# Re-dealing the lead-in of a transformer block: norm tiles, gates, gathers and an on-chip placement of the last tile

## What is computed

```python
x = x + L0_conv(ln_c(x))     # deformable attention with depthwise 3x3 convolutions
t = to_tokens(x); t = t + L0_ffn(ln_t(t)); x = from_tokens(t)
x = x + L1_conv(ln_c(x))     # large depthwise kernels, folded into one 7x7
t = to_tokens(x); t = t + L1_ffn(ln_t(t)); x = from_tokens(t)
```

## Time and profile before

| | us |
|---|---|
| median of 3 runs (least, most) | 1711.93 (1710.65, 1713.68) |
| the profiled execution | 1717.21 |
| its span, first to last instruction | 1715.4 |
| TensorE busy in it | 1422.9 (83%) |
| VectorE busy | 979.1 (57%) |
| ScalarE busy | 701.8 (41%) |
| GpSimd busy | 275.8 (16%) |

### The profile page before, as it was taken

The page is one execution under the profiler, slowest core; times in us unless marked ns, Lnnn a source line. Parts: engine busy times, 40 slices in busy tenths (PEclk is TensorE's granted clock), DMA queues, the critical chain, the costliest instruction groups (busy, mean ns, idle before and its releaser), DMA issues.

```text
span 1715.4 us, 19469 instructions
## 1 busy us (share of the span) xinstructions
PE 1422.9 (83%) x6076; PEld 958.6 (56%) x6076; DVE 979.1 (57%) x2678; ACT 701.8 (41%) x1433; POOL 275.8 (16%) x190
## 2 busy tenths in 40 slices
PE   4302528798777999998887999999999999999998
PEld 2201326555454577665555577666766676665565
DVE  4988777649896534448896544443434352244323
ACT  3210224335543234454543344454445443355443
POOL 2342115311162000001154000000000000000000
PEclk9999658898888999999888999999999999999999
DMA  3531304131342421331342422342224321221211
GB/s 100 129 95 46 105 20 116 53 111 57 90 120 52 122 67 51 95 112 61 106 103 59 129 67 52 93 120 70 71 64 114 98 66 48 71 69 42 69 61 45
DMA packets 169448, 137.96 MB, mean 80 GB/s; under 512 B 114688, under 2 KB 163074, under 8 KB 168962
## 3 DMA queue, kind: packets, MB, share of 16 engines
q1 hardware_dynamic: 162802, 131.26, 28.1%
q0 software_dynamic: 3072, 4.82, 1.2%
q10 hardware_dynamic: 3472, 0.63, 0.2%
HBM read 97.02 MB, written 39.65 MB: 80 GB/s over the span
## 4 chain that ended last, share of the span: by engine, by line
PE 50%; issue 19%; DVE 12%; POOL 8%; ACT 5%; DMA 3%; SPq 2%; ACTq 1%; POOLq 0%; DVEq 0%
PE y_ps L917 19%; PE at_ps L1020 8%; POOL pix_mem L837 6%; PE h_ps L926 5%; PE h_ps L925 5%; PE h_ps L924 5%; DVE vq_mem L1195 4%; PE at_ps L973 3%; POOL ln_rstd L824 3%; ACT ln_cen L689 2%; PE lb_ps L894 2%; PE lg_ps L907 1%; DVE part L1151 1%; DVE kon_mem L1195 1%; ACT hidden L784 1%
## 5 line engine op out<-in xcount | busy, mean ns | idle before, releaser
L784 ACT ACTIVATE hidden<-h_ps,b 128x448 f32<-128x448 f32 x672 | 424.6, 634 | 716.9 <-PE h_ps L926 714.0
L917 PE MATMUL y_ps<-hidden,w 128*96 128x448 f32 x1344 | 638.0, 559 | 29.6 <-ACT hidden L784 21.3
L924 PE MATMUL h_ps<-xh,w1h 96*128 96x448 f32 x672 | 474.4, 706 | 0.0
L1151 DVE SCALAR_TENSOR_TENSOR part<-y_ps,b,gate_t 96x448 f32<-96x448 f32 x224 | 151.8, 678 | 512.4 <-PE y_ps L917 472.4
L824 POOL TENSOR_TENSOR ln_rstd<-ln_ve,minus_half 112x4 f32<-112x4 f32 x112 | 156.0, 1393 | 1208.9 <-DVE ln_ve L1134 1208.7
L917 PEld LDWEIGHTS y_ps<-hidden,w 128*96 128x96 f32 x1344 | 207.4, 167 | 105.0 <-ACT hidden L784 59.5
L925 PE MATMUL h_ps<-xl,w1h 96*128 96x448 f32 x672 | 250.7, 373 | 0.0
L926 PE MATMUL h_ps<-xh,w1l 96*128 96x448 f32 x672 | 249.2, 371 | 0.0
L924 PEld LDWEIGHTS h_ps<-xh,w1h 96*128 96x128 f32 x672 | 130.5, 194 | 139.2 <-issue 122.9
L925 PEld LDWEIGHTS h_ps<-xl,w1h 96*128 96x128 f32 x672 | 131.8, 196 | 120.5 <-issue 119.7
L689 ACT ACTIVATE ln_cen<-ln_cen,ln_rstd 112x96 f32<-112x96 f32 x448 | 130.2, 363 | 160.7 <-POOL ln_rstd L824 160.5
(11 more groups left out here) (133 smaller groups left out, 1248.9 us busy)
## 6 DMA issues: line engine op xcount, KB each, us to landing
gate_t<-gates_dram SPq DMA_DIRECT2D x112, 336.0 KB, 3.1
value_pairs<-pix_mem SPq DMA_DIRECT2D x56, 168.0 KB, 3.1
x_mem<-norm_c SPq DMA_DIRECT2D x16, 420.0 KB, 4.2
x_mem<-norm_a SPq DMA_DIRECT2D x16, 336.0 KB, 3.8
ln_x<-in_x SPq DMA_DIRECT2D x28, 168.0 KB, 2.5
norm_a<-ln_cm SPq DMA_DIRECT2D x28, 168.0 KB, 2.3
res_mem<-in_x SPq DMA_DIRECT2D x4, 1176.0 KB, 9.8
x_attn<-res_mem SPq DMA_DIRECT2D x16, 294.0 KB, 2.9
```

The costliest lines, as they stand in the source:

```text
L784: act.activation(hidden[c % HID_RING][:, :], h_ps[c % H_BANKS][:, 0:TILE], ACT.Gelu, bias=b1[l][:, c:c + 1]).then_inc(gelu_done, 1)
L917: pe.matmul(y_ps[e % Y_BANKS][0:C, 0:TILE], w2[l][:, c, :], hidden[c % HID_RING][:, :], start=(j == 0), stop=(j == CPE - 1)).then_inc(hid_ ...
L924: pe.matmul(ps, hi, xh[:, ring(k)], start=True, stop=False)
L1151: dve.scalar_tensor_tensor(part[:, e, :], y_ps[e % Y_BANKS][0:C, 0:TILE], b2[l][:, e:e + 1], gate_t[e // 2][:, e % 2, :], ALU.add, ALU.mul ...
```

## The change

1. Lead-in: 13 steps in place of 15. Tiles 0 to 4 of a2 are normalised in steps 7 to 10, f0's tiles 0 to 3 in steps 10 to 12, f0's tiles 4 to 6 in (0, 0) and (0, 1), a2's tiles 5 and 6 in (0, 1) and (0, 2). Stage 3 of image 1 moves from step 13 to step 12. The first gate half is read in the last lead step, the second in (0, 1).
2. f0's tiles are turned in from `x_res` on the chip, once the strips they cover are added; they are no longer loaded. `x_res` of image 1 is loaded at stage 5 in place of 4, once all of them are turned.
3. The last tile of images 0, 2 and 3 goes from `ln_cm` straight into `xq` in three DMAs (`direct`); the fourth quarter's load leaves its rows out and is two DMAs.
4. In lead steps the second job's turn-in stands at chunk 8 (was 6), behind the first one's turn-back, and its apply at 9 (was 8).
5. Gathers: 4 in stage 3, 4 and 5 in stage 4, 3 in stage 5.
6. Ten of ScalarE's first loads go to SyncE's queue (4 ahead of the pads, 6 after step 0), four more to SyncE after step 1. `expand_w_out`, `spread_w_out` and `fold_taps` stand at the end of lead step 8.

```diff
-NORM_SLOT = {0: ("a", 2), 1: ("c", 0), ...
+NORM_SLOT = {1: ("c", 0), ...
-LEAD = 15
-START_JOBS = {... 6: [("a1", 5), ("a1", 6)], 11: [("f0", 0), ("f0", 1)], 12: [("f0", 2), ("f0", 3)],
-              13: [("f0", 4), ("f0", 5)], 14: [("f0", 6), ("a2", 0)]}
+LEAD = 13
+START_JOBS = {...
+              (-1, 6): [("a1", 5), ("a1", 6)], (-1, 7): [("a2", 0)], (-1, 8): [("a2", 1), ("a2", 2)],
+              (-1, 9): [("a2", 3)], (-1, 10): [("a2", 4), ("f0", 0)], (-1, 11): [("f0", 1), ("f0", 2)],
+              (-1, 12): [("f0", 3)], (0, 0): [("f0", 4), ("f0", 5)], (0, 1): [("f0", 6), ("a2", 5)],
+              (0, 2): [None, ("a2", 6)]}
-              11: [(1, 2)], 13: [(1, 3)]}
+              11: [(1, 2)], 12: [(1, 3)]}
...
-GATE_STEP = {(-1, LEAD - 2): (0, 0), (-1, LEAD - 1): (0, 1),
+GATE_STEP = {(-1, LEAD - 1): (0, 0), (0, 1): (0, 1),
...
-        TURN_IN = 1, 6
+        TURN_IN, LEAD_TURN_IN = (1, 6), (1, 8)
-        LEAD_APPLY, LEAD_BACK, LEAD_MOVE, LEAD_SCORES, LEAD_LATE_MOVE = (3, 8), 8, 9, 10, 4
+        LEAD_APPLY, LEAD_BACK, LEAD_MOVE, LEAD_SCORES, LEAD_LATE_MOVE = (3, 9), 8, 9, 10, 4
...
+                    if direct(job):
+                        for g in range(G):
+                            sp.dma_start(xq[Q - 1::Q, g, LAST_ROW * SIDE:LAST_ROW * SIDE + TILE],
+                                         ln_cm[job.n % 2][32 * g:32 * g + 32, :]).then_inc(xq_direct, 16)
+                        return
...
+                for r0, r1 in ((0, LAST_ROW), (ROWS_A - PAD_A, ROWS_A)) if split else ((0, ROWS_A),):
...
                 if 0 in stages and slot >= 0:
+                    load_quarter(stages[0], 2)
                     load_quarter(stages[0], 3)
...
-                if 4 in stages:
-                    b = stages[4]
+                if any(stage == (5 if b == 1 else 4) for stage, b in stages.items()):
+                    b = stages[5 if 5 in stages and stages[5] == 1 else 4]
...
+                    if b == 1:
+                        for job in PLACED:
+                            if from_attn(job):
+                                sp.wait_ge(ln_turned, job.n + 1)
...
                 if 4 in stages:
-                    gather(stages[4], 2, 6)
+                    gather(stages[4], 4, 8)
                 if 5 in stages:
-                    gather(stages[5], 10, 2 * GQ)
+                    gather(stages[5], 13, 2 * GQ)
                 if 1 in jobs:
                     scale_rows(jobs[1])
                 if 3 in stages:
-                    gather(stages[3], 0, 2)
+                    gather(stages[3], 0, 4)
                 if 4 in stages:
-                    gather(stages[4], 6, 10)
+                    gather(stages[4], 8, 13)
...
+                src = ln_x[n % 2]
+                if from_attn(job):
+                    src = x_res[:, tile_cols(job.tile)]
+                    pe.wait_ge(at_free, AT["attn", 0] + AT_Y + -(-(job.tile + 1) * TILE // YCOL))
+                else:
+                    pe.wait_ge(ln_loaded[n % 2], loads(n))
...
-                if (slot, p) == (1, 0):
+                if (slot, p) == (-1, 8):
+                    expand_w_out()
                     fold_taps()
```

More of the change, by code:

```diff
@@ L78 @@
 for _slot, _p in STEPS:
-    if _slot < 0:
-        _todo = [(what[0], int(what[1]), tile) for what, tile in START_JOBS.get(_p, [])]
+    if _slot < 0 or (_slot, _p) in START_JOBS:
+        _todo = [what and (what[0][0], int(what[0][1]), what[1]) for what in START_JOBS.get((_slot, _p), [])]
     elif _p <= 2:
@@ L88 @@
     JOBS[_slot, _p] = []
-    for _place, (_kind, _image, _tile) in enumerate(_todo):
+    for _place, (_kind, _image, _tile) in [(i, what) for i, what in enumerate(_todo) if what]:
         _job = Job(len(PLACED), _place, "f" if _kind == "f" else "c", _image, _tile,
@@ L376, in metaformer_kernel @@
         Q_ROUNDS = {4: (0, 9)}, {4: (0, 5), 5: (5, 8), 6: (8, 9)}
-        TURN_IN = 1, 6
+        TURN_IN, LEAD_TURN_IN = (1, 6), (1, 8)
         APPLY, BACK, MOVE, SCORES = 6, 7, 8, 9
         LATE_APPLY, LATE_BACK, LATE_MOVE, LATE_SCORES = 1, 2, 3, 5
-        LEAD_APPLY, LEAD_BACK, LEAD_MOVE, LEAD_SCORES, LEAD_LATE_MOVE = (3, 8), 8, 9, 10, 4
-        const_count, taps_count = [0], [0]
+        LEAD_APPLY, LEAD_BACK, LEAD_MOVE, LEAD_SCORES, LEAD_LATE_MOVE = (3, 9), 8, 9, 10, 4
+        const_count = [0]
         BAND_TILES = [3, 4, 6, 7]
         QUARTER_TILES = [2, 4, 6, 7]
+        XQ_LOADS = [sum(Q + (image in DIRECT) for image in range(b + 1)) for b in range(NB)]
+        LAST_ROW = PIX // TILE * TILE // SIDE - (Q - 1) * QROWS - TILE // SIDE + PAD_A
         CONV_STORE, ACC_LOAD = {}, {}
@@ L393, in norm_stores, with direct, from_attn, loads @@
         def norm_stores(norm, parity, tiles=TILES):
-            return 16 * sum(job.norm == norm and job.n % 2 == parity and job.tile < tiles for job in PLACED)
+            return 16 * sum(job.norm == norm and not direct(job) and job.n % 2 == parity and job.tile < tiles for job in PLACED)
+        def direct(job):
+            return job.norm is not None and job.norm[0] == "a" and job.norm[1] in DIRECT and job.tile == TILES - 1
+        def from_attn(job):
+            return job.kind == "f" and job.image == 0
+        def loads(n):
+            return 16 * sum(job.n % 2 == n % 2 and not from_attn(job) for job in PLACED[:n + 1])
         def f_count(job):
@@ L411, in metaformer_kernel @@
         block = ctx.enter_context(nc.Block())
+        r_w_a, r_b_a, r_w_c, r_w53, r_w35, r_w7, r_w5, r_b_c = views(rows_w)
+        tap_rows = [(dst, a[f"L1_conv_{w}"].rearrange("(g c) o h w -> c g (o h w)", g=G)) for dst, w in (
+            (r_w_c, "w77"), (r_w53, "w53"), (r_w35, "w35"), (r_w7[:, 0], "w7h"), (r_w7[:, 1], "w7w"),
+            (r_w5[:, 0], "w5h"), (r_w5[:, 1], "w5w"))]
+        tap_rows += [(r_b_c[:, n], a[f"L1_conv_{w}"].rearrange("(g c) -> c g", g=G))
+                     for n, w in enumerate(("b77", "b53", "b35"))]
+        N_TAPS = 9 + len(tap_rows)
         @block.sync
@@ L444, in load_constants, with load_tap_rows @@
                         const(gate_b[l][:, :], a[f + "gate_b"].partition_broadcast(SUB))
+            def load_tap_rows(n):
+                with nc.allow_non_contiguous_dma("small"):
+                    for dst, src in tap_rows[:n]:
+                        sp.dma_start(dst, src).then_inc(taps_ld, 16)
+                del tap_rows[:n]
             def load_norm(n):
                 job = PLACED[n]
+                if from_attn(job):
+                    return
                 if n >= 2:
@@ L592, in _ @@
                     load_norm(coming[0].n)
[L593 to L597, removed]
+                if slot < 0 and p == 3:
+                    load_quarter(0, 0)
+                    load_quarter(0, 1)
+                if 0 in stages and stages[0] > 0:
+                    for q in range(Q):
+                        if q < 2 or slot < 0:
+                            load_quarter(stages[0], q)
                 for job in LATE[slot, p]:
                     store_norm(job)
+                if slot < 0 and p == 3:
+                    load_quarter(0, 2)
+                    load_quarter(0, 3)
                 if 0 in stages and slot >= 0:
+                    load_quarter(stages[0], 2)
                     load_quarter(stages[0], 3)
@@ L699, in move @@
                     act.wait_ge(split, f_count(before) + 1)
+                elif before is not None and direct(before):
+                    act.wait_ge(xq_direct, 16 * G * (DIRECT.index(before.image) + 1))
                 elif before is not None:
@@ L883, in turn_in @@
                 for s in range(NSUB):
-                    last = pe.transpose(lt_ps[0:SUB, s * C:(s + 1) * C], ln_x[n % 2][:, s * SUB:(s + 1) * SUB],
+                    last = pe.transpose(lt_ps[0:SUB, s * C:(s + 1) * C], src[:, s * SUB:(s + 1) * SUB],
                                         ident[0:C, 0:C])
@@ L1042, in _ @@
                     for job in JOBS[slot, p]:
-                        if c == TURN_IN[job.place]:
+                        if c == (TURN_IN if slot >= 0 else LEAD_TURN_IN)[job.place]:
                             turn_in(job)
@@ L1433, in _ @@
                     dve.wait_ge(taps_set, 1)
-                    expand_w_out()
                 if by_stage.get(0) == 3:
@@ L1453, in _ @@
                     if at == 0 and till > 0 and 0 in by_stage:
-                        dve.wait_ge(xq_ld, 16 * Q * (by_stage[0] + 1))
+                        dve.wait_ge(xq_ld, 16 * XQ_LOADS[by_stage[0]])
+                        dve.wait_ge(xq_direct, 16 * G * sum(image <= by_stage[0] for image in DIRECT))
                     for op in ops[at:till]:
```

56 lines of the change are left out of this document (29 added, 27 removed), and 3 rows, old and new, of the table START_JOBS.

## The result

Five runs of the changed kernel took 1703.64 us in the median (1700.06 to 1706.79), beside 1712.92 us (1710.65 to 1715.71) for five of the kernel before: ratio 0.9947, 95% interval 0.9927 to 0.9967. That is faster by 9.3 us, where 26.9 were forecast, and 1703.64 lies outside 1670 to 1702. The profiled execution took 1700.06 us (span 1698.2), the fastest of the five; that of before, 1717.21 us, was above all five of its timed runs.

A forecast was written before the change was run, and what follows sets the result against it. VectorE was taken to bound the lead-in and image taps, TensorE the last two thirds. Terms: lead-in -7.0, then -0.5, -2.6, -11.0, -2.4, -3.4, sum -26.9 us from 1711.93: 1685 us, range 1670 to 1702.

The forecast's parts named there:

- (a) Start: Lead-in up to the first taps (46.22 us before): earlier first apply, but slower turn-in pairs; +1.0 us (-2 to +3).
- (b): Lead-in, 46 to 141 us: waits at the twelfth and fourteenth tiles, two added tiles of image 2; +7.3 us.
- (c): Lead-in, 141 to 187 us: four more normalisations, expand_w_out, fold_taps and about 2 us of small waits; +16.8 us.
- rival 2: Taps hold GpSimd back; the 16th tile's rstd waits for the query burst's end: +3.8 us, 1689 us; chance 10 in 100.
- three signs: First combine at 275 us or later; rstd before query taps ending behind them; early TensorE clock nearer 0.5 than 0.9.
- (d): Lead-in, 187 to 271 us: less VectorE work, tiles read from x_res; 84.2 becomes 52.1 us, -32.1 us.
- Slot 0: FFN steps behind the lead-in: extra VectorE work against a shorter wait for image 1's pixels; net -0.5 us (-3.7 to +2).
- Direct last tile: Without the store and load, quarter-row waits shrink: -2.6 us for image 2's rows, -2.4 us for image 3's.
- fold_taps and gathers at image 2: Without fold_taps there, 6.3 us earlier; three gathers fewer cover the 4.68 us wait: -11.0 us (-6.3 to -11).
- Gathers: Re-dealt gathers; at image 3, three fewer behind the rstd cut the 4.99 us wait to about 1.6: -3.4 us.
- Rival 3: Re-dealt gathers give nothing, delaying turn-backs as much as the waits shrink: 1697 us; chance 12 in 100.
- Rival 1: The lead-in gives nothing; serialised turn-ins and moved work fill what its tail frees: 1692 us; chance 20 in 100.

The follow-up runs named there:

- the third run: Changed kernel with the lead's second turn-in back at chunk 6 and its apply at 8, except in step 10: median 1695.03 us, ratio 0.9885.
- the tenth run: Changed kernel with only image 0's last tile direct, those of images 2 and 3 stored and loaded again: median 1700.93 us, ratio 0.9927.
- The seventh run: Changed kernel with fold_taps moved back to step (1, 0): median 1702.5 us, ratio 0.9945.
- the sixth: Changed kernel with the gathers dealt as before the change (2, then 4 and 4, then 6): median 1713.45 us, ratio 0.9999.
- the ninth: Kernel before the change with only the new gather deal (4, 4 and 5, 3): median 1703.77 us, ratio 0.9944.
- The three edits: Changed kernel with step 10's apply behind the m copies, one gather fewer before image 0's 16th rstd, turn-in at chunk 6 except step 10: 1687.77 us.
- The eighth: Changed kernel with apply behind m copies, turn-in at chunk 6 except step 10, fold_taps before the query burst, gathers 6, 3, 4, 3 for images 1 to 3: 1684.86 us.
- eleventh: The eighth with the changed kernel's gathers (4, 4, 5, 3) at images 2 and 3: median 1684.66 us, ratio 0.983.
- The fourth: The three edits together on the changed kernel: median 1687.77 us, ratio 0.9862, first combine at 268.26 us.

## Why the prediction was wrong

**(a) Start: right.** 47.80 us, forecast 47.2; a pair takes 8.74 us, forecast 8.75. The term of +1.0 is a difference: the new order costs 7.4 us by the third run, and without it the first taps would have come 5.8 us ahead of the 46.22 of before.

**(b): right.** The burst ends at 150.6 us, forecast 149.3. The twelfth tile waits 2.61 us (forecast 2.8), the fourteenth 1.57 (1.65).

**(c): the step that failed.** 73.9 us from there to the last strip, forecast 63.0. Its "about 2 us of new small waits" were 13 us: 3.83 (rival 2) and 7.30 and 1.9 ahead of strips. Two of the three signs that the prediction had named for being wrong came with it, the late first combine and the rstd that ends behind the query taps. Rival 2 I priced well and gave 10 in 100, on the strength of gathers that passed the burst and of one rstd ahead of a different one-input form. With five rstds newly placed beside taps, that each would find a gap was the unlikely case. The other stall is the omission: of the tile moved into step 10 I counted VectorE's four instructions and GpSimd's one, and did not write down the queue of ScalarE around the apply.

**(d): right.** 53.6 us, forecast 52.1. The largest term and the one I trusted least held.

**Slot 0: right in sum** (first combine +6.2, tile (0, 2) +6.2, forecast -0.5), by exchange of one wait for another.

**Direct last tile: half right.** The waits shrank by 2.6 and 2.3 us as forecast, but the tenth run gives to it only 0.8 and 1.5, so the match is in part luck.

**fold_taps and gathers at image 2: right.** Between (1, 0) and (1, 2) the traces show -10.9 us, forecast -11.0. The seventh run gives 6.2 of them to fold_taps (forecast 6.3), the sixth 3.8 and the ninth 4.7 to the gathers (forecast 4.7). The 2.9 us more up to (1, 3) are a clock drop (below). In the whole the move of fold_taps gives nothing, since the lead pays for it.

**Gathers: right in sum.** -8.6 us for images 1 to 3 in my terms (-0.5, -4.7, -3.4), 9.4 by the median of the ninth run. At image 3 the traces show -4.0 (-3.5 by the sixth run). In the changed kernel they also keep 3.5 us in the lead, which I had nowhere. Rival 3, that they give nothing, was the furthest from the truth in its mechanism, though rivals 1 and 3 together, 1704, have the measured time: that is luck. Rival 1, that the lead gives nothing, was the nearest in mechanism: 1692 was its time, and the lead took 6 us more than nothing.

The sum was wrong by 17.6 us in the medians, and 13.2 of them are the lead: +6.2 in place of -7.0. Behind it the traces show -23.3 us, -17.9 without the clock drops, where -19.9 were forecast; some 2 us between traces and medians stay open. The three edits put the first combine where the forecast had it, and with them the ratio is 0.9862 where 1685 meant 0.984.

## What to carry to other kernels

When a step is moved, write down for every engine in its chain what is queued behind it, not only what it costs: two stalls of 3.8 and 7.3 us came from an apply and a turn-in that stood ahead of urgent work, and another order cured both without making the slow instruction faster. Work moved between two places in which the same engine is full is worth nothing; and when a change bundles many parts, run the cheapest part alone, since here the numbers in four calls held all of the gain.

## What the runs showed of the hardware

**GpSimd's small instruction and VectorE's bursts.** An rstd of 1.01 us took 5.96, 12.71, 23.20 and 25.51 us beside 5, 13, 24 and 27 large taps. It ends 0.9 us behind the burst in each, whether it is issued behind the start of the two-input taps (128.36) or 0.3 us ahead of the burst (47.51, 126.31, 195.62). Large taps are not the only ones: beside 14 two-input taps of 128x196 (0.34 us each) and two splits of an FFN tile it took 6.96 and ended 0.9 us behind them too.

```profile
236.28 6.96 POOL L870 TENSOR_TENSOR ln_rstd<-ln_ve,minus_half 112x4 f32<-112x4 f32 x1 [9.31 <-DVE ln_ve L1185]
```

```profile
236.58 4.72 DVE L1246 SCALAR_TENSOR_TENSOR kon_mem<-x_mem,all_w,kon_mem 128x196 f32<-128x196 f32 x14
241.22 1.15 DVE L1193 TENSOR_TENSOR xl<-ln_cm,xh 96x448 fp32r<-96x448 f32 x2
```

Beside the 36 small instructions of fold_taps (128x7 and 128x5, 0.14 us each) it took 1.05. It took 1.05 too in the changed kernel when issued at 169.76 us, 0.29 us ahead of two two-input instructions of 98x768 (0.96 us each). So size alone does not decide which instructions hold it, and what does was not tried.

**Clock drops.** In two stretches of 10 us the granted clock of the kernel before falls to 0.67 (part of the stretch at 1.2 GHz, the rest at 2.4), and at the same tiles of the changed kernel's profile it is 1.00 (columns: length, TensorE's busy time, clock, DMA share, GB/s):

```profile
580.00:590.00 10.00, 8.21 (x26) 0.67 0.36 110
...
1560.00:1570.00 10.00, 9.86 (x30) 0.67 0.10 35
```

The tile times jump there, by 2.9 us from (1, 2) to (1, 3) and 2.6 from (6, 4) to (6, 5). The eighth and eleventh runs' profiles have the first again and pay 3.0 us at the same tile, which I had put down to their deal. The eighth:

```profile
560.00:570.00 10.00, 9.61 (x37) 0.66 0.22 64
```

The fourth, which pays nothing at that tile:

```profile
560.00:570.00 10.00, 8.11 (x44) 1.00 0.45 123
```

So 5.5 of the 17.15 us between the two traces are drops. That would be most of the 7.9 us that the medians do not show, if the other runs had as many drops in either kernel, for which there is no trace. What brings one on was not settled: the changed kernel's other runs, at 1702.57 to 1706.79 us, have a mean granted clock of 0.96 against the profiled one's 0.931, so the mean alone does not order the times.
